# A four-layer spectral mixing kernel: the order of its load queue, and of the work around the last flipped inverse

## What is computed

```python
# layers 0, 2, 3: real Fourier transform over (H, W); k are the modes
o1r = relu(xr @ w1[0] - xi @ w1[1] + b1[0]); o1i = relu(xi @ w1[0] + xr @ w1[1] + b1[1])
o2r = o1r @ w2[0] - o1i @ w2[1] + b2[0];     o2i = o1i @ w2[0] + o1r @ w2[1] + b2[1]
out = irfft2(softshrink(o2r) + 1j * softshrink(o2i)) + x
# layer 1: Hartley transform over image AND channels AND batch
X_k = dht(x); X_nk = x flipped in H and W
s = softshrink(o2_k + o2_nk)      # the same kind of mixing, of X_k and X_nk
out = dht(s) / s.size + x
```

## Time and profile before

| | |
|---|---|
| median of three runs | 1125.68 us (1125.51 to 1128.65) |
| the profiled execution | 1123.99 us, its span 1122.2 us |
| TensorE busy | 942.2 us, 84% |
| VectorE / ScalarE / GpSimd busy | 575.4 / 475.5 / 75.4 us |
| mean granted TensorE clock | 0.919 of full |
| bytes moved | 184.39 MB, mean 164 GB/s |
| chain that ended last | TensorE 72%, transfers 14%, VectorE 4%, SP's queue 3% |

### The profile page before, as it was taken

The page is one execution under the profiler, slowest core; times in us unless marked ns, Lnnn a source line. Parts: engine busy times, 40 slices in busy tenths (PEclk is TensorE's granted clock), DMA queues, the critical chain, the costliest instruction groups (busy, mean ns, idle before and its releaser), DMA issues.

```text
span 1122.2 us, 14252 instructions
## 1 busy us (share of the span) xinstructions
PE 942.2 (84%) x5168; PEld 480.4 (43%) x5168; DVE 575.4 (51%) x869; ACT 475.5 (42%) x757; POOL 75.4 (7%) x148
## 2 busy tenths in 40 slices
PE   2889977996999680999999977999999999999702
PEld 1546544654656550833444433444443344344301
DVE  2255541453444660558867553666666666665401
ACT  1444442442444320243434431665555555556401
POOL 1011110111011010000001011000000000000000
PEclk8899996998999895599999997999999999999956
DMA  8887694578267678284343613344465384451452
GB/s 304 290 269 252 179 314 150 152 197 297 75 199 237 162 230 153 76 188 115 92 130 92 157 43 95 94 122 110 117 210 172 107 262 134 153 190 46 141 151 113
DMA packets 95695, 184.39 MB, mean 164 GB/s; under 512 B 12487, under 2 KB 74081, under 8 KB 93834
## 3 DMA queue, kind: packets, MB, share of 16 engines
q1 hardware_dynamic: 86442, 144.17, 45.4%
q0 software_dynamic: 9184, 39.30, 10.6%
HBM read 104.29 MB, written 79.14 MB: 163 GB/s over the span
## 4 chain that ended last, share of the span: by engine, by line
PE 72%; DMA 14%; DVE 4%; SPq 3%; issue 3%; ACT 2%; POOL 0%; ACTq 0%; DVEq 0%; POOLq 0%
PE psum L862 15%; PE psum L871 14%; PE psum L901 7%; PE psum L954 6%; PE psum L978 5%; PE psum L912 5%; DMA RG<-rows_along_h 5%; PE psum L850 4%; PE psum L938 4%; DMA rows_along_h<-RD 4%; PE psum L881 4%; DMA RX<-rows_along_w 3%; PE psum L965 3%; PE psum L827 2%; SPq L561 2%
## 5 line engine op out<-in xcount | busy, mean ns | idle before, releaser
L1275 DVE SCALAR_TENSOR_TENSOR RA<-psum,RA 112x896 f32<-112x896 f32 (+1 forms) x120 | 124.1, 1034 | 240.8 <-ACT RA L1130 240.8
L1130 ACT ACTIVATE RA<-psum,small 112x896 f32<-112x896 f32 (+1 forms) x120 | 115.8, 965 | 98.7 <-PE psum L871 98.2
L871 PE MATMUL psum<-RA,RW 112*64 112x448 f32 (+1 forms) x640 | 133.3, 538 | 2.7 <-ACT RA L1121 2.7
L1121 ACT ACTIVATE RA<-psum,RW 112x448 f32<-112x448 f32 (+1 forms) x160 | 89.2, 609 | 88.0 <-PE psum L862 88.0
L912 PE MATMUL psum<-const,RG 128*96 128x66 f32 x512 | 61.5, 290 | 65.4 <-DMA RG<-rows_along_h 56.6
L901 PE MATMUL psum<-RD,const 128*128 128x384 f32 (+1 forms) x304 | 99.6, 449 | 10.2 <-DVE RA L1235 5.5
L1235 DVE COPY RD<-psum 128x672 f32<-128x672 f32 (+2 forms) x120 | 68.4, 572 | 67.3 <-PE psum L901 63.6
L1115 ACT ACTIVATE RN<-psum 96x264 f32<-96x264 f32 (+4 forms) x52 | 30.4, 584 | 157.7 <-PE psum L912 105.1
L912 PEld LDWEIGHTS psum<-const,RG 128*96 128x96 f32 x512 | 58.7, 204 | 73.8 <-DMA RG<-rows_along_h 57.7
L1115 ACT ACTIVATE RA<-psum 128x384 f32<-128x384 f32 (+2 forms) x72 | 50.6, 702 | 89.6 <-PE psum L850 51.4
L850 PE MATMUL psum<-const,RX 128*112 128x128 f32 x528 | 69.3, 284 | 19.8 <-DMA RX<-rows_along_w 19.8
(11 more groups left out here) (99 smaller groups left out, 1080.6 us busy)
## 6 DMA issues: line engine op xcount, KB each, us to landing
RG<-rows_along_h SPq DMA_DIRECT2D x6, 3072.0 KB, 11.1
rows_along_w<-RX SPq DMA_DIRECT2D x64, 224.0 KB, 5.0
rows_along_h<-RD SPq DMA_DIRECT2D x96, 144.0 KB, 2.8
RX<-x SPq DMA_DIRECT2D x16, 768.0 KB, 7.9
out<-RA POOLq DMA_DIRECT2D x16, 768.0 KB, 4.3
rows_along_h<-RD SPq DMA_DIRECT2D x64, 168.0 KB, 2.9
RX<-rows_along_w SPq DMA_DIRECT2D x12, 672.0 KB, 6.7
spectrum<-RA POOLq DMA_DIRECT2D x48, 168.0 KB, 4.7
```

Source lines behind the costliest of these rows:

```text
L871: mm = nc.tensor.matmul(bank[b * HALF:(b + 1) * HALF, a * BANK:a * BANK + nk * H], w4[layer][0:ROWS, g, b, a], hidden(slot)[0:ROWS, b * N: ...
L1121: done = nc.scalar.activation(hidden(slot)[0:ROWS, b * N:b * N + nk * H], banks(key)[0:ROWS, b, 0:nk * H], ACT.Relu, bias=bias[layer][0:RO ...
L1130: nc.scalar.activation(dst, src, ACT.Relu, bias=minus_lambda_l0 if key[0] == "S4" else minus_lambda).then_inc(act_emptied, 1)
L1275: nc.vector.scalar_tensor_tensor(out=dst, in0=src, scalar=LAMBDA / 64 if key[0] == "S4" else LAMBDA, in1=dst, op0=ALU.add, op1=ALU.min).th ...
```

## The change

The flipped inverse of passes 0 and 1 starts one round later, 6C of pass 2 three rounds later. Item 0's H1 and H2 are put in front of the last pass's 6A, whose G is then loaded in one transfer. SP stores turned rows first in a round, loads y(0) and y(1) in round 36 and y(2) in round 38 (all three were in 37), and VectorE sums them one step later. Layer 2's weights (load_conv) are loaded behind G and y(3). The last G of phase C is still loaded in two parts, but the first holds the columns of three groups (20 of 32 rows) and is issued two rounds earlier; the last holds 12 rows. Half of pass 0's stage stores are issued by GpSimd.

```diff
@@ -82,11 +82,11 @@
 
 
 def flip_round(p):
-    return 10 * p + 18
+    return 10 * p + (18 if p == PASSES - 2 else 19)
 
 
 def last_inverse_round(p):
-    return 10 * p + (16 if p < PASSES - 2 else 18)
+    return 10 * p + (16 if p < PASSES - 2 else 21)
 
 
 def order():
@@ -119,8 +119,10 @@
         if 0 <= r - ALL_STEPS - 4 < 2:
             o += [("CF", 0, r - ALL_STEPS - 4)]
     o += [("CF", 1, h) for h in range(2)]
+    for h in range(2):
+        o += [("H1", 0, 2 * h), ("H1", 0, 2 * h + 1), ("H2", 0, h)]
     o += [("6A", PASSES - 1, g, v) for g in range(PASS_PAIRS) for v in range(FLIP_UNITS)]
-    for z in range(ITEMS + 2):
+    for z in range(1, ITEMS + 2):
         if z < ITEMS:
             o += [("H1", z, 0), ("H1", z, 1)]
         if z < ITEMS:
@@ -448,6 +450,7 @@
         pads_zeroed = sem("pads_zeroed")
         x_loaded = [sem(f"x_loaded{k}") for k in range(X_PARTS)]
         stage_stored = [sem(f"stage_stored{s}") for s in range(STAGE_SLOTS)]
+        first_stage_stored = [sem(f"first_stage_stored{k}") for k in range(X_PARTS)]
         bm_loaded = [sem(f"bm_loaded{s}") for s in range(BM_SLOTS)]
         turned_stored = [sem(f"turned_stored{s}") for s in range(TURN_SLOTS)]
         g_loaded = [sem(f"g_loaded{s}") for s in range(2)]
@@ -494,7 +497,10 @@
 
         def wait_stage_stored(eng, p, k):
             m = p * X_PARTS + k
-            eng.wait_ge(stage_stored[m % STAGE_SLOTS], 64 * (m // STAGE_SLOTS + 1))
+            halves = sum(n % STAGE_SLOTS == m % STAGE_SLOTS for n in range(min(m + 1, X_PARTS)))
+            eng.wait_ge(stage_stored[m % STAGE_SLOTS], 64 * (m // STAGE_SLOTS + 1) - 32 * halves)
+            if p == 0:
+                eng.wait_ge(first_stage_stored[k], 32)
 
         def wait_bm_loaded(eng, e):
             eng.wait_ge(bm_loaded[e % BM_SLOTS], 16 * (e // BM_SLOTS + 1))
@@ -503,7 +509,7 @@
             eng.wait_ge(turned_stored[e % TURN_SLOTS], 64 * (e // TURN_SLOTS + 1))
 
         def g_uses(p):
-            return sum(16 * (8 if m % PASSES == PASSES - 1 else 1) for m in range(p % 2, p + 1, 2))
+            return sum(16 * (8 if m == 2 * PASSES - 1 else 1) for m in range(p % 2, p + 1, 2))
 
         def wait_flipped_stored(eng, p, g):
             m = p * PASS_PAIRS + g
@@ -542,6 +548,11 @@
         def edges_of(s):
             return 2 if step_of(s)[0] == 0 else 0
 
+        def stage_views(p, k, x):
+            at = (4 * k + x) * X_HP
+            return (rows_along_w[p, at:at + X_HP].rearrange("y q r -> q y r"),
+                    stage(p, k)[x * HP:(x + 1) * HP].rearrange("q (y r) -> q y r", r=PASS_ROWS))
+
         block = ctx.enter_context(nc.Block())
 
         @block.sync
@@ -553,19 +564,17 @@
             def load_x(p, k):
                 sp.dma_start(X(k), x[p, k]).then_inc(x_loaded[k], 16)
 
-            def store_stage(p, k):
+            def store_stage(p, k, parts):
                 wait_emptied(sp, ("S1", p, 2 * k))
                 wait_emptied(sp, ("S1", p, 2 * k + 1))
-                for x in range(4):
-                    at = (4 * k + x) * X_HP
-                    sp.dma_start(rows_along_w[p, at:at + X_HP].rearrange("y q r -> q y r"),
-                                 stage(p, k)[x * HP:(x + 1) * HP].rearrange("q (y r) -> q y r", r=PASS_ROWS)
-                                 ).then_inc(stage_stored[(p * X_PARTS + k) % STAGE_SLOTS], 16)
+                for x in range(parts):
+                    dst, src = stage_views(p, k, x)
+                    sp.dma_start(dst, src).then_inc(stage_stored[(p * X_PARTS + k) % STAGE_SLOTS], 16)
 
             def load_bm(e):
                 p, q, _, _ = group_of(e)
                 if q == 0:
-                    for k in range(1, X_PARTS):
+                    for k in range(X_PARTS):
                         wait_stage_stored(sp, p, k)
                 lo, hi = columns_of(e)
                 sp.dma_start(Bm(e), rows_along_w[p, :, lo:hi]).then_inc(bm_loaded[e % BM_SLOTS], 16)
@@ -594,12 +603,12 @@
                 sp.dma_start(G(p), src).then_inc(g_loaded[p % 2], 16)
 
             def load_g_part(p, last):
-                e = PASS_GROUPS * (p + 1) - 2 + last
+                e = PASS_GROUPS * (p + 1) - (2 if last else 4)
                 if not last:
                     wait_g_free(p)
-                    wait_turned_stored(sp, e - 1)
-                wait_turned_stored(sp, e)
-                split = columns_of(PASS_GROUPS * (p + 1) - 1)[0]
+                for turn in (e, e + 1):
+                    wait_turned_stored(sp, turn)
+                split = columns_of(PASS_GROUPS * (p + 1) - 2)[0]
                 lo, hi = (split, HP) if last else (0, split)
                 for x in range(4):
                     sp.dma_start(G(p)[x * HP + lo:x * HP + hi], rows_along_h[p, x, lo:hi]).then_inc(g_loaded[p % 2], 16)
@@ -653,7 +662,7 @@
                 sp.dma_start(a[0:ROWS, W3 + W4:], conv_bias[n]).then_inc(conv_loaded[n], 16)
 
             for k in range(X_PARTS):
-                store_stage(0, k)
+                store_stage(0, k, 2)
             for e in range(BM_SLOTS):
                 load_bm(e)
             for k in range(X_PARTS):
@@ -664,30 +673,30 @@
             load_prep("va0", l1_w3)
             sp.dma_start(fwd_c, fwd_c_dram).then_inc(fwd_loaded, 16)
             for r in range(A_ROUNDS):
+                if r % 2 == 1 and 0 <= (r - 7) // 2 < ALL_GROUPS:
+                    e = (r - 7) // 2
+                    for part in range(2):
+                        wait_emptied(sp, ("5A", e, part))
+                    store_turned(e)
                 for p in range(1, PASSES):
                     k = r - first_transform_round(p)
                     if 0 <= k < X_PARTS:
-                        store_stage(p, k)
+                        store_stage(p, k, 4)
                         if p + 1 < PASSES:
                             load_x(p + 1, k)
                 e = (r + 4) // 2
                 if r % 2 == 0 and BM_SLOTS <= e < ALL_GROUPS:
                     wait_filled(sp, ("S2", 2 * (e - BM_SLOTS) + 1))
                     load_bm(e)
-                if r % 2 == 1 and 0 <= (r - 7) // 2 < ALL_GROUPS:
-                    e = (r - 7) // 2
-                    for part in range(2):
-                        wait_emptied(sp, ("5A", e, part))
-                    store_turned(e)
-                for p in range(PASSES):
-                    if p < PASSES - 1 and r == 10 * p + 16:
+                for p in range(PASSES - 1):
+                    if r == 10 * p + 16:
                         load_g(p)
-                    elif p == PASSES - 1 and r == 10 * p + 14:
-                        load_g_part(p, 0)
-                if r == 37:
+                if r == 36:
                     sp.wait_ge(zero_stored, 16 * B)
-                    for m in range(Y_SLOTS):
+                    for m in range(B):
                         load_y(m)
+                if r == 38:
+                    load_y(B)
                 if r == 41:
                     wait_filled(sp, ("6A", 2, PASS_PAIRS - 1, FLIP_UNITS - 1))
                     sp.dma_start(v3, first_mix).then_inc(mix_loaded, 16)
@@ -696,10 +705,10 @@
                     for g in range(PASS_PAIRS):
                         wait_flipped_stored(sp, 1, g)
                     load_an(0)
+            load_g(PASSES - 1)
+            load_y(3)
             wait_filled(sp, ("S4", ALL_STEPS - 1))
             load_conv(1)
-            load_g_part(PASSES - 1, 1)
-            load_y(3)
             wait_filled(sp, ("6A", PASSES - 1, PASS_PAIRS - 1, FLIP_UNITS - 1))
             for g in range(PASS_PAIRS):
                 wait_flipped_stored(sp, PASSES - 1, g)
@@ -745,7 +754,7 @@
                 for p in range(PASSES):
                     if p < PASSES - 1 and r == 10 * p + 15:
                         load_g(PASSES + p)
-                    elif p == PASSES - 1 and r == 10 * p + 13:
+                    elif p == PASSES - 1 and r == 10 * p + 11:
                         load_g_part(PASSES + p, 0)
             load_g_part(2 * PASSES - 1, 1)
 
@@ -766,6 +775,12 @@
             pool.wait_ge(zero_set, 1)
             for i in range(B):
                 pool.dma_start(spectrum[i, FOLD].rearrange("k a h -> k (a h)"), zeros).then_inc(zero_stored, 16)
+            for k in range(X_PARTS):
+                wait_emptied(pool, ("S1", 0, 2 * k))
+                wait_emptied(pool, ("S1", 0, 2 * k + 1))
+                for x in range(2, 4):
+                    dst, src = stage_views(0, k, x)
+                    pool.dma_start(dst, src).then_inc(first_stage_stored[k], 16)
             nc.gpsimd.memset(prep["w4"][0:ROWS], 0.0).then_inc(prep_zeroed, 1)
             nc.gpsimd.memset(prep["v"], 0.0).then_inc(prep_zeroed, 1)
             for r in range(A_ROUNDS):
@@ -1423,10 +1438,10 @@
                         wait_filled(vec, ("5A", e - D_SLOTS, 1))
                     wait_filled(vec, key)
                     copy(*turn_views(key, 0)).then_inc(vec_emptied, 1)
```

(4 more changed lines are left out.)

## The result

| | before | after |
|---|---|---|
| median (range), four runs each | 1125.60 us (1125.27 to 1128.65) | 1066.88 us (1063.45 to 1068.31) |
| span of the profiled execution | 1122.2 us | 1065.0 us |
| mean granted TensorE clock | 0.919 | 0.943 |
| chain that ended last: TensorE / transfers | 72% / 14% | 75% / 12% |

The ratio is 0.9469, with an interval of [0.945, 0.9489]: 58.7 us faster, 5.3%. The direction was forecast, the size was not: 1048 us, a gain of 77.5, was predicted, and the measured median lies 4 us above the range's upper end of 1063. One execution, in experiment 5, came out at 1380.36 us with a mean granted clock of 0.646, where every other had 0.912 or more; its experiment is given without it.

The account below looks back on a forecast made before the run. TensorE was taken to bound the kernel, with 99 of 1122 us idle in waits for G and VectorE. Savings of 1 + 16 + 14 + 9.5 + 24 + 13 = 77.5 us gave 1048 us, range 1036 to 1063.

Parts of the forecast that it names:

- part 4: Middle: item 0 ahead of the last 6A, G loaded whole; item 1 starts at 462.2 instead of 486.46, saving 24 us.
- rivals of the other sign: Whole kernel slower (0.02): SP waits in odd rounds for 5A's copies, making Bm late; takes over at 4.1 us per round.
- G stays late in the rounds: Rival for the rounds (0.10): stage, x and y transfers share G's ring, 12 to 15 us of waits stay, 1061 us.
- Part 1, start: Start: half of pass 0's stage stores move to GpSimd's queue, 1 us saved, bounds -2 to +3.
- Part 2, rounds: Rounds 15 to 29: turned rows stored first, 6A of passes 0 and 1 one round later; 16 and 14 us saved.
- load_g issues near 156.5, G lands at 168.5: First wait for G: earlier issue meets 6A's demand at 168.5, leaving 1.5 us of wait; 16.0 us saved.
- The second wait: Rounds, 6A's next wait for G: none of its 11.0 us stays and low clock gives 3, so 14.0 saved.
- Part 3, y sums: Rounds 36 to 40: y loads one round earlier, their sums one later, 9.5 us saved.
- its favourable bound: Middle: 28 us saved instead of 24, with 6A at full clock.
- Part 5, tail: Tail: last load split 20 + 12 rows, first part earlier, pass 2's 6C later; 13 us saved, between 0 and 16.5.
- the last store lands at 1069: Tail: the last turned store lands at 1069, between 1065.6 and 1079, instead of 1082.07.
- 28 to 30 by bytes: Tail rival (0.08): the last part's load goes by its bytes and takes 28 to 30 us, not 14.9; +14, 1062 us.

Follow-up runs that it names:

- experiment 5: Changed kernel with the last G of phase C loaded in one transfer behind the last turned store: 1053.28 us (three runs), ratio 0.9345.
- Experiment 1: Changed kernel with SP again issuing all 16 stage stores of pass 0: 1067.54 us, ratio 0.9462.
- Experiment 2: Changed kernel with load_g of passes 0 to 2 put ahead of the same round's Bm load in SP's order: 1057.24 us, ratio 0.9354.
- experiment 3: Changed kernel with 6A of passes 0 and 1 placed another round later (20 and 30): 1050.68 us, ratio 0.9303.
- Experiment 4: Changed kernel with turned stores again behind stage stores, x and Bm in SP's order, 6A still one round later: 1070.07 us, ratio 0.9482.
- experiments 7 and 8: 7: changed kernel with item 0 behind the last 6A again, G whole, 1072.63 us. 8: changed kernel with half of item 0 on either side, 1065.03 us.
- second joined kernel: Changed kernel with all stage stores on SP, 6A of passes 0 and 1 one round later, last G whole, pass 2's 6C behind the loop: 1034.96 us.
- experiment 6: Changed kernel with 6C of pass 2 starting in round 38 again, last G still loaded as 20 + 12 rows: 1069.04 us, ratio 0.9493.

## Why the prediction was right and wrong

**Direction: right, and the mechanism in the middle and for the y sums.** Every wait of 6A and 6C that was named shrank, the new wait for an(1) came with about the size forecast (9.6 against 9.4, partly by luck, as part 4 shows), and none of the rivals of the other sign took place. The rival that came nearest is "G stays late in the rounds", given 0.10 and priced at 12 to 15 us; it cost 14. Its stated mechanism, transfers sharing the ring with G, was half of the truth. It did not come alone, so that even its 1061 was too low.

**Part 1, start: the term's sign failed.** It was taken as 1 us saved with -2 to +3 as bounds. The case named as a bound, the first part's store landing 2 us later because GpSimd's stores share the engines, is what happened (the copies behind it start at 21.25 against 18.65). The -3.1 of the profile lies outside the bound of -2; 1.9 of it are the low clock behind a later wait for Bm, which the split does not always bring and which also came without it. Experiment 1 has both back in its trace; the medians do not resolve it.

**Part 2, rounds: the failing step is "load_g issues near 156.5, G lands at 168.5".** The demand was right: 6A was ready at 172.03, which less the 3.06 of the start is 168.97, against 168.5. On the same scale G was issued at 160.3, 3.8 us late, since I had let SP pass from stage store to x to Bm by their issue times and overlooked in load_bm that the first group of a pass waits for the stage stores to land; and it took 14.43 us in company instead of 12. Together 6.2 us, less the 0.5 by which the demand came later: that is the wait of 5.8, for which 1.5 had been kept. With a wait left, the 4.1 us of low clock behind it did not come back either: 16 became 8.5. The second wait went the same way, 13.42 us of load, 3.48 of wait, 7.8 instead of 14. Experiment 2 takes the Bm wait away and returns 4 and 6 us; experiment 3 takes the wait itself away and returns 11 and 7. Experiment 4 shows that the reordering, which the prediction took to be half of this part, gives 1 us at most: the 3.5 us of earlier issue are paid back by a transfer that takes 2.5 us more.

**Part 3, y sums: right**, 9.7 against 9.5: VectorE's wait for y fell from 7.5 us to 0.3 and 6A's wait for its copy went with it. No run undid this part alone.

**Part 4, middle: the load's part right, the end at its favourable bound for another reason.** Put on the clock of before by the 22.92 us gained until CF, item 0 starts at 419.4 as said and 6A at 431.7 (432). 6A ends at 447.1 instead of 451, the an load follows by 5.9 (5.9) and lands 3.6 later (3.5). I had argued from the earlier trace rows that 6A does not raise the clock by itself. That is so, as experiments 7 and 8 show again, but it enters with the clock of what stands in front of it, and item 0 ran at 2.4 GHz. Yet what then sets the time is VectorE, whose last copy is what the store of the flipped rows waits for. The prediction had its work at 18 us from 433, ending at 451; it took 15.1 (432.9 to 448.0), because the eight copies cost 4.0 us and not 5, and the join of y, 2.1, stands behind the last copy and so outside it. In all nine traces with item 0 in front of 6A this copy ends 37.7 to 37.8 us after the last 24 matmuls of CF begin, whether the last two units of 6A took 5.38, 4.79 or, in the second joined kernel, 2.93 (a row of its timeline, then two of its chain):

```profile
399.10 2.93 PE L916 MATMUL psum<-const,RG 128*96 128x66 f32 x32 [1.59 <-DVE RN L1239]
...
404.45 0.96 DVE RN L1239 x2
...
405.70 4.59 DMA flipped<-RN
```

There the an load follows 6A's end by 8.4 us and TensorE waits 12.2, and item 1 starts no earlier. So the agreement of the 5.9, and of 9.6 with 9.4, is luck: the load goes by VectorE's last copy, 5.0 us behind it in both. The low clock on item 1's first H1 cost 2.8 (5.99 in the chain against 3.20), not 1.8. What moving item 0 was worth the prediction did not say, but its numbers do: with G at 430, then 6A for 20.75 and item 0 for 14.1, item 1 would start at 464.9 instead of 462.2, 2.7 later; experiment 7 gives 2.5.

**Part 5, tail: the step "the last store lands at 1069" failed.** The first part was issued where forecast (1046.8 on the clock of before), and the 12 rows cost what 6 rows cost: 15.6 us with issue, against 14.9 forecast and 28 to 30 by bytes. The Trainium skill (DMA: Bandwidth & Descriptors, Why a DMA increments its semaphore by 16 and not by 1) lets 12 rows use 12 engines where 6 rows use 6; the two durations agree with it. But the store landed at 1075.3 on that scale: issued at 1063.0, it took 12.27 us, where the forecast left it 6. I had reckoned the queue to need the 21.1 us of before and 1 more; it needed 28.5, with two turned stores and four out stores of 768 KB beside the first part. Experiment 5 shows that without the first part it takes 4.81 us, and that the whole of G behind it is then still 3 us faster than the last 12 rows alone. So the split, whose last part was priced rightly, was itself the loss: neither rows nor bytes tell why four transfers of 12 rows take longer than one of 4 x 32, and no run here settles it. Three units out of the loop gave 1.9 us by experiment 6, against 2.0.

**The range.** Its upper end, 1063, held one rival at a time. The two errors share a root: I priced a transfer by the time of a row in which it ran in other company, once for G (2.4 of its 6.2 us; the other 3.8 are the overlooked wait) and once for the store. A common root of several terms belongs in the range as one case with its sum: 14 + 6 on top of 1048 would have covered the result.

## What to carry to other kernels

Before you credit a load with an earlier issue, go through the issuing queue instruction by instruction and read in the code what each one waits for, not only how long it takes to issue; and price the transfer in the company that it will then have, for here a load issued 3.5 us sooner arrived 1 us sooner. Moving the consumer by one more unit of work that costs nothing was worth more than all reordering of the queue. When work is moved to fill a wait, count what it had been hiding where it stood: item 0 filled the wait for G and uncovered the one for an(1), and 2.5 us were gained in all. Where a wait cannot be removed, look at the clock of the work behind it, and ask which engine ends the stretch before crediting the faster clock: 6A ran 5.4 us faster behind item 0, and VectorE set the end.

## What the runs showed of the hardware that I had not expected

- 6A's 128 matmuls of 66 columns ran at 1.4 us per unit of 16 when H1 and H2 stood directly before them at 2.4 GHz, and at 2.6 us per unit, for 20.75 us without a gap, when a wait of 2.58 or 8.09 us stood before them. In nine traces a wait of 1.59 us in their midst was followed by 2.93 us for the last two units in two, 4.79 in three and 5.38 in four.
- The same code with the same wait (2.7 us before a 5A) kept 2.4 GHz in eight executions and lost it in four, at a cost of 1.4 to 3.0 us. So a single profile does not settle an effect of 3 us here.
- The price of a small strided part of a load does not go by its bytes: four transfers of 6 rows took 13.89 us, of 12 rows 14.42 and 14.63, but one of 4 x 32 rows 11.39, with the engines moving some 400 GB/s throughout.
- Giving half of a burst of stores to a second queue made the first part, on which the next work waited, land 2.6 us later, with the DMA share at 0.99 (10 to 15 us) and 1.05 (18 to 21). The half on SP's queue landed at 21.22 us, the half on GpSimd's at 17.45; before, on SP's queue alone, all had landed by 18.63.
